# One transformer layer with eight experts on one core: wider expert regions, one register load per tile, pads between tiles, scatters that wait for tile counts, three expert tiles per row of maxima

## The reference

```
logits = einsum('bsh,eh->bse', x, Wr);  probs = softmax(logits)
top_v, top_i = top_k(probs, 2);         top_v = top_v / sum(top_v)
for e in range(8):
    w_e = sum(where(top_i == e, top_v, 0))
    h = gelu(einsum('bsh,mh->bsm', x, W1[e]) + b1[e])      # 128 -> 512, erf gelu
    y = einsum('bsm,hm->bsh', h, W2[e]) + b2[e]            # 512 -> 128
    out = out + y * w_e
x = layernorm(x + out)
```

## Time and profile before

| | us |
|---|---|
| median of 3 runs | 783.81 |
| lowest and highest | 782.26, 784.75 |
| the profiled execution's own time | 781.19 |
| its span (first to last instruction) | 779.4 |
| PE busy | 653.2 (84%) |
| DVE, ACT, POOL busy | 481.4, 380.4, 319.7 |
| granted TensorE clock, mean of the span | 0.932 |

### The profile page before, as it was taken

How to read it: one execution, slowest core, us unless ns; L and a number is a source line. 1 busy time by engine, 2 the same in 40 slices (tenths; PEclk the granted TensorE clock), 3 DMA queues, 4 the chain that set the end, 5 groups by cost and what they waited for, 6 DMA issues and landing times.

```text
span 779.4 us, 19919 instructions
## 1 busy us (share of the span) xinstructions
PE 653.2 (84%) x6134; PEld 495.3 (64%) x6134; DVE 481.4 (62%) x1626; ACT 380.4 (49%) x786; POOL 319.7 (41%) x464
## 2 busy tenths in 40 slices
PE   9879898898899998998998988887897874679780
PEld 8664656756755755854764764666886764678780
DVE  4587568778768668679669687763662443233345
ACT  0212465475474475475375475454554532344453
POOL 6104362363363354364264254146323253233355
PEclk7579999999999999999999999999997996899985
DMA  8300000000000000000000000325453242445663
GB/s 299 93 1 14 2 33 12 1 28 14 1 24 14 3 24 14 3 24 14 3 21 14 7 21 11 118 73 164 125 162 96 80 132 63 135 148 164 200 223 135
DMA packets 36142, 52.90 MB, mean 68 GB/s; under 512 B 8552, under 2 KB 19561, under 8 KB 35946
## 3 DMA queue, kind: packets, MB, share of 16 engines
q1 hardware_dynamic: 30936, 42.23, 17.7%
q0 software_dynamic: 4576, 9.53, 3.5%
q10 hardware_dynamic: 578, 0.53, 0.2%
HBM read 40.64 MB, written 12.63 MB: 68 GB/s over the span
## 4 chain that ended last, share of the span: by engine, by line
PE 44%; DVE 16%; issue 13%; POOL 7%; ACT 6%; SPq 4%; another core or an unknown queue 3%; DMA 3%; DVEq 1%; ACTq 1%; POOLq 1%
PE bank L1770 8%; PE bank L2095 5%; PE bank L2079 4%; PE bank L1935 4%; PE bank L1806 4%; ACT mix L616 3%; POOL rstd L828 3%; PE bank L1923 3%; PE bank L1904 3%; PE bank L1855 3%; PE bank L1863 2%; PE bank L1693 2%; PE bank L1943 2%; DVE negmax L1294 1%
## 5 line engine op out<-in xcount | busy, mean ns | idle before, releaser
L869 POOL DMA_INDIRECT expert_in<-xb_rows,slot_u x72 | 73.0, 1014 | 107.4 <-PE bank L1913 49.0
L730 ACT ACTIVATE kT<-bank,w1c 128x128 f32<-128x128 f32 x192 | 54.8, 370 | 75.3 <-PE bank L2079 39.7
L1294 DVE TENSOR_REDUCE negmax<-bank 128x4 f32<-128x512 f32 x128 | 79.6, 681 | 7.1 <-PE bank L1904 7.1
L2079 PE MATMUL bank<-xqT,w1c 128*128 128x128 f32 x568 | 79.7, 285 | 1.8 <-DVE xqT L1542 1.6
L825 POOL TENSOR_SCALAR vare<-mv 128x1 f32<-128x1 f32 (+1 forms) x107 | 24.1, 225 | 138.4 <-DVE mv L1173 137.7
L2095 PE MATMUL bank<-x_all,kT 128*128 x384 | 59.8, 305 | 23.4 <-ACT kT L730 12.1
L616 ACT ACTIVATE mix<-bank 128x512 f32<-128x512 f32 x128 | 66.0, 604 | 23.1 <-PE bank L1923 23.1
L2079 PEld LDWEIGHTS bank<-xqT,w1c 128*128 128x128 f32 x568 | 73.1, 201 | 3.6 <-DVE xqT L1542 2.0
L2095 PEld LDWEIGHTS bank<-x_all,kT 128*128 128x128 f32 x384 | 53.0, 214 | 28.4 <-issue 28.3
L828 POOL TENSOR_TENSOR rstd<-vare,minus_half 128x1 f32<-128x1 f32 (+1 forms) x107 | 65.3, 610 | 9.4 <-POOL vare L825 1.1
L955 POOL DMA_INDIRECT expert_out<-hebT,v_sb x35 | 34.0, 970 | 77.0 <-DVE hebT L1555 55.5
(11 more groups left out here) (325 smaller groups left out, 1461.5 us busy)
## 6 DMA issues: line engine op xcount, KB each, us to landing
w1c<-in_w_t SPq DMA_DIRECT2D x71, 258.0 KB
v_sb<-expert_in SPq DMA_DIRECT2D x71, 66.0 KB
x_all<-in_x SPq DMA_DIRECT2D x4, 512.0 KB, 7.8
xT_all<-in_xT SPq DMA_DIRECT2D x4, 512.0 KB, 8.3
ctxT<-in_ctxT SPq DMA_DIRECT2D x8, 256.0 KB
x_all<-in_w_t SPq DMA_DIRECT2D x1, 2048.0 KB, 7.3
mix<-expert_out SPq DMA_DIRECT2D x4, 512.0 KB, 4.8
back_rows<-expert_out SPq DMA_DIRECT2D x4, 512.0 KB, 3.7
```

Of the source, the lines that this page charges most:

```text
L730: ins = nc.scalar.activation(hx[j % HX][:, c, :], bank[HIDDEN_BANKS[j % 2]][:, c * P:(c + 1) * P], ACT.Gelu, bias=w1c[j % W1B][:, FF + c:F ...
L869: nc.gpsimd.indirect_dma_start(xs[:, :], bass.IndirectOffsetOnAxis(ap=slot_u[:, t, k:k + 1], axis=0), xb_rows[k][:, t, :], None).then_inc( ...
L1294: nc.vector.tensor_reduce(negmax[t % 2][:, i, 28:28 + XC], b[:, :].rearrange("p (c n) -> p c n", c=XC), AX.X, ALU.max, negate=True).then_i ...
L2079: ins = mm(bank[HIDDEN_BANKS[j % 2]][:, c * P:(c + 1) * P], w1c[j % W1B][:, c * P:(c + 1) * P], xtT[j % 4], start=True, stop=True)
```

## The change

- REGION becomes 8192 rows instead of 5120. The region number of a row is then the row shifted right, so one register load per tile is enough: `tile_in(j)` loads the row number, issues the rows, then computes the expert from the same register and issues the weights.
- `pad(eng, e)` does one pad. SP waits for `ends_ready` before tile 36 (PADS_AT) and issues two pads ahead of each of the tiles 36 to 39, where before all eight stood behind tile 40.
- POOL: `paced(ins_of, tiles)` waits until `h_mm` has reached a count of tiles, then issues. The 16 `row_out` of the last section and `results_out` of tiles 24, 26, 28 and 30 and 31 to 48 are given such counts, and the last group's 8 `row_out` alternate with `results_out`.
- PE, DVE and ACT: three expert tiles (three `hidden`, two `outputs`) stand in each round of maxima instead of four and three. In all 18 hidden tiles stand ahead of attention instead of 22; two more are put inside attention; the two output banks are used from tile 27 on instead of 31.

The core of the diff:

```diff
-REGION = (SEQS + EXP) * P
+REGION = 8192
-BACK_AT = 66
+PADS_AT, BACK_AT = 36, 66
-ONE_OUT, OUT_BANKS = 31, (3, 4)
+ONE_OUT, OUT_BANKS = 27, (3, 4)
...
-            def weights_in(j):
-                n, nth_tile = batch_of(j)
-                e = sp.value_load(tab[n][0:1, 0, nth_tile:nth_tile + 1], min_val=0, max_val=EXP - 1)
-                if j >= W1B:
-                    sp.wait_ge(gelu_done, j - W1B + 1)
-                    sp.sem_inc(sp_held, 1)
-                sp.dma_start(w1c[j % W1B][:, :], A["w1_t"][:, bass.ds(e, 1), :].rearrange("p a n -> p (a n)")
-                             ).then_inc(x_in[j % ROWS], 16)
-
-            def row_in(j):
+            def tile_in(j):
                 n, nth_tile = batch_of(j)
                 row = sp.value_load(tab[n][0:1, 1, nth_tile:nth_tile + 1], min_val=0, max_val=EXP * REGION - P)
...
                 sp.dma_start(rows_sb[:, j % ROWS, :], xs[bass.ds(row, P), :]).then_inc(x_in[j % ROWS], 16)
+                if j >= W1B:
+                    sp.wait_ge(gelu_done, j - W1B + 1)
+                    sp.sem_inc(sp_held, 1)
+                sp.dma_start(w1c[j % W1B][:, :], A["w1_t"][:, bass.ds(row // REGION, 1), :].rearrange(
+                    "p a n -> p (a n)")).then_inc(x_in[j % ROWS], 16)
...
-            for j in range(TA):
-                row_in(j)
-                weights_in(j)
+            for j in range(PADS_AT):
+                tile_in(j)
             sp.wait_ge(ends_ready, 1)
-            pad(sp)
+            for j in range(PADS_AT, TA):
+                for e in range(2 * (j - PADS_AT), min(2 * (j - PADS_AT) + 2, EXP)):
+                    pad(sp, e)
+                tile_in(j)
...
+            def paced(ins_of, tiles):
+                pool.wait_ge(h_mm, tiles)
+                pool.sem_inc(pool_held, 1)
+                ins_of()
             g = G - 1
-            for t in range(2):
-                for k in range(TOPK):
-                    row_out(t, k)
+            row_out(0, 0)
+            paced(lambda: row_out(0, 1), 1)
+            paced(lambda: row_out(1, 0), 2)
             for t in range(T):
                 ln_scale(LNA, g, t)
...
+            paced(lambda: row_out(2, 0), 5)
+            results_out(1)
             output_bias(g)
+            paced(lambda: row_out(2, 1), 6)
...
+            paced(lambda: row_out(3, 0), 9)
+            paced(lambda: row_out(3, 1), 12)
...
             rows_chosen(g)
             for t in range(T):
-                for k in range(TOPK):
-                    row_out(t, k)
+                paced(lambda: row_out(t, 0), 26 + 3 * t)
+                results_out(23 + 2 * t)
+                paced(lambda: row_out(t, 1), 27 + 3 * t)
+                paced(lambda: results_out(24 + 2 * t), 28 + 3 * t)
+            for j in range(31, 49):
+                paced(lambda: results_out(j), 38 + 2 * (j - 31) // 3)
...
             for t in range(T):                       # PE
                 max_scores(g, t)
-                hidden(6 + 4 * t)
-                outputs(5 + 3 * t)
-                hidden(7 + 4 * t)
-                outputs(6 + 3 * t)
-                hidden(8 + 4 * t)
-                outputs(7 + 3 * t)
+                hidden(6 + 3 * t)
+                outputs(5 + 2 * t)
+                hidden(7 + 3 * t)
+                outputs(6 + 2 * t)
+                hidden(8 + 3 * t)
                 turn_max(g, t)
-                hidden(9 + 4 * t)
```

More of the change, by code:

```diff
@@ L420, in settled, with pad @@
             eng.wait_ge(free[b], g * PER_GROUP[b] + (NTH_FIRST[name] + 2))
-        def pad(eng):
-            for e in range(EXP):
-                n_pad = 1 if e < EXP - 1 else EXP
-                end = eng.value_load(ends_i[0:1, e:e + 1], min_val=e * REGION, max_val=e * REGION + SEQS * P)
-                rows = xs[bass.ds(end, n_pad * P), :]
-                eng.dma_start(rows.bitcast(U32), A["spare"][e * P:(e + n_pad) * P, :]).then_inc(padded, 16)
+        def pad(eng, e):
+            n_pad = 1 if e < EXP - 1 else EXP
+            end = eng.value_load(ends_i[0:1, e:e + 1], min_val=e * REGION, max_val=e * REGION + SEQS * P)
+            rows = xs[bass.ds(end, n_pad * P), :]
+            eng.dma_start(rows.bitcast(U32), A["spare"][e * P:(e + n_pad) * P, :]).then_inc(padded, 16)
         def batch_of(j):
@@ L751, in _ @@
             placed_queries(g, 2)
-            for j in range(5, 22):
+            for j in range(5, 18):
                 gelu(j)
@@ L763, in _ @@
             gelu_table()
-            gelu(22)
+            gelu(18)
             drain(g, "cxT", cxT[:, :])
-            for j in range(23, 27):
+            for j in range(19, 23):
                 gelu(j)
@@ L769, in _ @@
             second_rows(g)
-            for j in range(27, NORMS_AT + 5):
+            for j in range(23, NORMS_AT + 5):
                 gelu(j)
@@ L974, in _ @@
                 ln_scale(LNB, g, t)
-            for j in range(23, 26):
+            for j in range(18, 22):
                 results_out(j)
             second_ratio(g)
+            results_out(22)
             rows_chosen(g)
             for t in range(T):
-                for k in range(TOPK):
-                    row_out(t, k)
+                paced(lambda: row_out(t, 0), 26 + 3 * t)
[4 more added lines that the diff above has]
+                paced(lambda: results_out(j), 38 + 2 * (j - 31) // 3)
             def last_scale(g):
@@ L990, in last_scale @@
                                         ).then_inc(rstdc_ready, 1)
-            for j in range(26, TILES):
+            for j in range(49, TILES):
                 results_out(j)
@@ L1591, in _ @@
                 maxima(g, t, range(0, 2))
-                results_of(5 + 3 * t)
-                pair_in(4 + 2 * t)
+                results_of(5 + 2 * t)
+                if t % 2 == 0:
+                    pair_in(4 + 3 * t // 2)
                 maxima(g, t, range(2, 4))
-                results_of(6 + 3 * t)
-                results_of(7 + 3 * t)
+                results_of(6 + 2 * t)
                 shifted(g, t)
-                pair_in(5 + 2 * t)
-            for j in range(17, 22):
-                results_of(j)
+                pair_in(5 + 3 * t // 2)
+            results_of(13)
+            results_of(14)
+            results_of(15)
+            pair_in(10)
+            results_of(16)
             for t in range(T):
                 normalise(g, t)
-            pair_in(12)
-            results_of(22)
+            results_of(17)
+            results_of(18)
+            pair_in(11)
             dve.wait_ge(xab_ready, G)
@@ L1657, in shift @@
                                                ).then_inc(shiftc_ready, 1)
-            for j in range(32, TILES):
+            for j in range(28, TILES):
                 if j % 2 == 0 and j // 2 + 2 <= (TILES - 1) // 2:
@@ L2149, in _ @@
             turn_context(g, 3)
+            outputs(17)
+            turn_heads(g)
+            outputs(18)
+            hidden(20)
+            cross_outputs(g)
+            outputs(19)
+            hidden(21)
+            outputs(20)
             hidden(22)
-            turn_heads(g)
+            outputs(21)
+            turn(g, "xbT", LNB, g, xb)
             hidden(23)
             outputs(22)
-            cross_outputs(g)
+            routes(g)
             hidden(24)
@@ L2157, in _ @@
             hidden(25)
+            ranks(g)
             outputs(24)
-            hidden(26)
-            outputs(25)
-            turn(g, "xbT", LNB, g, xb)
-            hidden(27)
-            outputs(26)
-            routes(g)
-            hidden(28)
-            outputs(27)
-            hidden(29)
-            ranks(g)
-            outputs(28)
-            for j in range(29, TILES):
+            for j in range(25, TILES):
                 if j + 1 < TILES:
```

51 lines of the change are left out of this document (27 added, 24 removed).

## The result

| | before | after |
|---|---|---|
| median (runs) | 784.03 (4) | 754.24 (4) |
| lowest and highest | 782.26, 784.75 | 752.60, 757.13 |
| ratio, 95% interval | | 0.9627 [0.9591, 0.9664] |
| profiled execution | 781.19 | 753.08 |
| its span, granted clock | 779.4, 0.932 | 751.3, 0.943 |

The account below looks back on a forecast made before the run. Bounds: POOL's scatter runs holding PE's signals, then SP's loads. `ranks` at 612.8 plus 114.1 ends PE at 726.9 (-33.0); span 746.4, plus 1.8 and 2.6, forecast 751. Own range 739 to 763; 8 in 10, 736 to 769.

Parts of the forecast that it names:

- the last two terms: End of the run: 19.5 us behind PE's last tile left as is, then 1.8 and 2.6 from span to median.
- Scatters at the start: POOL near 537 us: six row scatters in a row become at most two; -4.5 us, bounds 0 and -6.5.
- Rounds of maxima: Four rounds, each a hidden and an output tile less on PE; -8.0 us, bounds -5 and -9.
- Attention: ACT's wait for third key scores shrinks (-3.5), exponentials begin earlier (-1.5); -5.0 us together, bounds -2 and -6.5.
- nothing behind it: Behind attention: a later gelu (+0.5) and layer norm scales freed from a result scatter (-0.5), nothing together.
- The 47 tiles: Output tiles 24 to 70: 34 at 2.1 us, 13 at 2.3; 101.3 us together, bounds 89 and 114.
- the late loads: Allowance for a run of four scatters and late loads, as once between 691 and 703 us; +4.5 us.
- reading back: Output tiles 61 to 66, the four reads unmoved: 15.8 us for five tiles instead of 10.5; +5.3 us.
- Pads: SP, two ahead of each of tiles 36 to 39: a stall of 3.0 instead of 6.45 + 11.8, bounds 0 and 7.
- the second rival: The tail stays at 2.43 us a tile, through SP's computed expert number or DMA; +11, 762 us; chance 0.15.
- the first: Rival: scatters don't hold PE's signals, or pacing doesn't cure it; +16, 767 us; chance 0.14.
- the loop: Rival: held result scatters delay DVE's drains and PE, so POOL's awaited hidden tiles come late; 802 us, chance 0.05.

Follow-up runs that it names:

- x4: The kernel before with all of the change except the order of tiles on PE, DVE and ACT (four per round kept), counts set later; 770.37 us, ratio 0.9897.
- b4: The kernel before with only the rounds of three tiles and POOL's places of the results between the norms; 775.30 us, ratio 0.9982.
- m1: The kernel before with two awaited memsets on POOL behind each of the last section's eight row scatters; 773.20 us, ratio 0.9928.
- x3: The kernel after, its order of scatters kept, but none waits for a count of hidden tiles; 746.88 us, ratio 0.9587.
- c1: The kernel after with only the first eight row scatters waiting for no count of hidden tiles; 746.87 us, ratio 0.9601.
- the control: The kernel after, unchanged, run again on another chip beside other kernels; 749.02 us, ratio 0.9646 to before.
- x1: The kernel after with a second register load per tile (the expert number) put back on SP; 760.92 us, ratio 0.9774.
- d3: c1 with results 31 to 48 unpaced, four pads on SP ahead of tiles 34 to 37, four on ACT, last row scatters 2.5 tiles apart; 746.54 us, 0.9548.
- x2: The kernel after with all eight pads in a row behind tile 40 again; 755.72 us, ratio 0.9671.

## Why the prediction was right

The time came within 4 us, in part by errors that cancel: D was 9.5 us longer than its term and what follows 6.4 shorter, `ranks` came 3.0 late, and the last two terms were 2.7 too high. That these nearly cancel is luck. The parts were priced one by one, and x4 and b4 show that about 18 of the 28 us can't be laid to either part alone.

- *Scatters at the start*, -4.5: stretch A gave -6.9. The cause (an unbroken run) holds by m1, the cure that I named (the counts) doesn't, by x3 and c1. "POOL's six in a row become at most two" was the failing step: the counts delay the rows, and what piles up behind them is a run of its own. It cost 5 to 6 us in the first round of the profile after, 1 to 2 in that of the control (8.9 us against c1's 7.7 and the forecast's 6.75); the bounds had no room for that above 0. In D the run indeed didn't grow: the kernel after has at most three scatters in a row there until 660 us, x3 has seven.
- *Rounds of maxima*, 6.75 each: 6.75 and 6.85 where nothing disturbed them.
- *Attention*, -5.0, and nothing behind it: C gave -5.9. `ranks` was forecast for 612.8 and came at 615.81, all of the gap and more in the first round; in the control at 609.95, or 612.1 on the scale of before, as its last group began 2.1 us earlier.
- *The 47 tiles*: this sum was mis-sized in two places. D was put at 12 x 2.1 + 6 x 2.3 + 3.0 = 42.0 and measured 51.5. I priced its tiles by PE; x4, with four tiles fewer in 51.1, and m1, with 47.8 by pauses on POOL alone, speak for POOL and SP as what sets it, without showing how much each does. What follows, tiles 42 to 70, was put at 7 x 2.3 + 22 x 2.1 + 5.3 + 4.5 = 72.1 and measured 65.7: tiles 49 to 60 did take 2.10, but the late loads that I kept from before (4.5) didn't come, and output tiles 61 to 66 took 12.8 us (711.23 to 724.01) instead of 15.8, against +5.3 for reading back.
- *Pads*, a stall of 3.0 at 1.2 us a pad: between loads a pad cost (5.2 - 1.8) / 2 = 1.7 us, and the stall was 5.6 with a slow clock behind it, near the upper bound of 7.
- *Register load*: the second rival's price, 11 us for a tail at 2.43, is what x1 measured, 10.
- *The range*: 751 with 6 back for weak rounds and attention and 4 for pads is 761, not 763; nothing hangs on it.
- *What lies around*: G was 18.3 instead of 19.5, and the median stood 2.9 above the span instead of 4.4.

Of the rivals, the first was half right: the scatters are what holds the signals, but the pacing wasn't the cure. The tail didn't stay at 2.43, and the loop didn't start. That the parts are worth little by themselves was in none of the cases; as all of the change was applied, it didn't hurt the forecast.

## What to carry to other kernels

Where a stretch has its own chain (routing, scatters, pads, the first load that needs them), price it by that chain's engines and not by the tile rate of TensorE alone. Work moved under such a chain can be free (after against x4) or not (b4), so read which wait ends last there. A long run of indirect DMAs is broken by what stands between them, and a wait that delays one piles up the next: look at what is queued behind it. Two changes that each gain 1% or less may gain 3.5% together, so a part tried alone and found worthless isn't settled.

## What the runs showed of the hardware

- While POOL issued indirect DMAs 1.27 us apart without a pause, ACT and DVE stood idle for up to 13.11 and 10.58 us until a remote release that came 0.5 us ahead of the run's end to 1.4 behind its last scatter (before), though PE's tiles were done; the same in b4 (10.29 and 10.43 us), x3 (6.29 and 5.46) and after (3.79 and 4.25). With two memsets between the scatters, 2.4 us from one to the next, no idle time ended so (m1), and it came back there with nine scatters in a row (8.01). Four in a row sufficed for a start 3.1 us late (d3). Why this is so stays open.
- A pad (a DMA from DRAM to DRAM with a register load) held SP for 1.2 to 1.3 us in a row of eight (9.65 us before, 10.43 in x2) and, by an estimate from the distance of loads in after, for 1.7 between tiles' loads.
- After waits of 2.37 us (d3), 3.42 us (after, 551.59) and 5.60 us (after, 650.18) PE came back at the lower clock: eight matmul records of an output tile took 2.07 us instead of 1.06. It didn't after every such wait: 1.15 us behind one of 3.68 (m1, 669.46).
